# Two empty steps in the node stream of the last phase: one ahead of the second moments, one ahead of the shares

## The reference, cut to what matters

```python
out = agg.reshape(N, HEADS * HEAD_DIM) + xn @ W_res + bias
out = layer_norm(out, ln2_g, ln2_b)
ff = gelu_tanh(out @ ffn_w1 + ffn_b1) @ ffn_w2 + ffn_b2
x = x + out + ff                       # end of the attention layer
z = layernorm(x)
w = softmax(z @ Wr + br)               # shares of the 8 experts, per node
for e in experts:                      # h1, h2: relu(batchnorm(. @ W + b))
    y += w[:, e] * (h2(h1(z)) @ Wo[e] + bo[e])
x = x + y
```

## Time and profile before

| | |
|---|---|
| median of 3 runs | 3436.0 us (3429.38 to 3451.61) |
| the profiled execution | 3452.29 us, span 3450.7 us |
| mean granted TensorE clock | 0.898 of full speed |
| busy share of the span | PE 81%, DVE 64%, POOL 50%, ACT 44% |
| last phase | from about 1620 us to 3450.7 us |

### The profile page before, as it was taken

One profiled execution on the slowest core, in us unless ns is written; L12 is line 12 of the kernel. 1 busy time (PEld: TensorE's weight loads), 2 busy tenths in 40 slices (PEclk: granted clock), 3 DMA queues, 4 the chain that ended last, 5 costly groups with the idle time before them and its releaser, 6 DMA issues.

```text
span 3450.7 us, 51683 instructions
## 1 busy us (share of the span) xinstructions
PE 2781.1 (81%) x17241; PEld 2488.3 (72%) x17241; DVE 2193.0 (64%) x5199; ACT 1527.7 (44%) x2928; POOL 1731.8 (50%) x1691
## 2 busy tenths in 40 slices
PE   8468777677867777665468889999899999999998
PEld 7346666566756656565468888888788888898887
DVE  9424444444444444764567787887878878878754
ACT  5102222222222223333135656666566666566665
POOL 0466666656666654263555555555555445554200
PEclk9879988898889889687569899999999999999999
DMA  3645554545555544047657877777767768677544
GB/s 94 190 148 174 159 157 148 154 145 164 157 157 157 156 146 128 1 144 218 183 171 232 255 230 223 242 217 226 239 210 243 234 209 246 214 230 229 160 127 139
DMA packets 369271, 625.87 MB, mean 181 GB/s; under 512 B 86045, under 2 KB 237599, under 8 KB 368995
## 3 DMA queue, kind: packets, MB, share of 16 engines
q1 hardware_dynamic: 290659, 407.24, 37.2%
q0 software_dynamic: 75168, 211.78, 21.5%
q10 hardware_dynamic: 3168, 3.42, 0.3%
HBM read 508.86 MB, written 113.37 MB: 180 GB/s over the span
## 4 chain that ended last, share of the span: by engine, by line
PE 32%; DVE 12%; issue 6%; ACT 3%; DMA 1%; another core or an unknown queue 1%; SPq 0%; POOL 0%; DVEq 0%; ACTq 0%
PE PB L117 25%; DVE WGl L2443 2%; PE PB L2124 2%; PE PB L2126 2%; DVE G L2437 1%; PE PB L2139 1%; DVE XR L2616 1%; DVE H1l L2604 1%; ACT WGh L2290 1%; PE PB L2187 1%; DMA RI<-resd 1%; ACT TFm L2363 1%; DVE AR L2482 0%; DVE H2l L2604 0%
## 5 line engine op out<-in xcount | busy, mean ns | idle before, releaser
L2095 POOL DMA_INDIRECT G<-tab,SRCL x784 | 864.6, 1103 | 775.3 <-DVE WGl L2443 550.7
L900 POOL DMA_INDIRECT G<-tab,SRCL x782 | 768.4, 983 | 481.9 <-issue 224.5
L2363 ACT ACTIVATE TFm<-PB,BIA,SCL 128x512 f32<-128x512 f32 (+2 forms) x416 | 312.9, 752 | 241.6 <-PE PB L117 187.4
L932 PE MATMUL PB<-G,OR 128*128 128x257 f32 x782 | 272.8, 434 | 96.4 <-DMA G<-tab,SRCL 40.9
L2290 ACT CAST WGh<-G 128x1056 fp32r<-128x1056 f32 x196 | 210.4, 1073 | 290.8 <-DVE G L2437 144.4
L117 PE MATMUL PB<-H1h,MW 128*128 128x512 f32 (+2 forms) x832 | 297.8, 399 | 31.5 <-DVE H1l L2604 20.2
L117 PE MATMUL PB<-MW,H2h 128*128 128x256 f32 x1568 | 295.0, 286 | 16.6 <-DVE H2l L2604 14.0
L117 PE MATMUL PB<-YTMh,MW 128*128 128x512 f32 (+2 forms) x832 | 289.2, 397 | 1.3 <-ACT TF L2328 0.8
L2124 PE MATMUL PB<-WGh,OR 128*128 128x264 f32 x784 | 223.2, 310 | 59.2 <-DVE WGl L2443 32.5
L933 PE MATMUL PB<-G,OR 128*128 128x257 f32 x782 | 266.7, 426 | 0.0
L117 PEld LDWEIGHTS PB<-MW,H2h 128*128 128x128 f32 x1568 | 244.6, 191 | 23.5 <-DVE H2l L2604 14.8
(11 more groups left out here) (348 smaller groups left out, 7901.0 us busy)
## 6 DMA issues: line engine op xcount, KB each, us to landing
MW<-msplit SPq DMA_DIRECT2D x312, 512.0 KB
ord<-OR SPq DMA_DIRECT2D x392, 128.0 KB
OR<-ord SPq DMA_DIRECT2D x196, 256.0 KB
ROW<-relrow SPq DMA_DIRECT2D x196, 128.0 KB
G<-tab,SRCL POOLq DMA_INDIRECT x1566
msplit<-FWs SPq DMA_DIRECT2D x68, 256.0 KB
tab<-ACC SPq DMA_DIRECT2D x7, 896.0 KB, 7.4
resd<-RSG SPq DMA_DIRECT2D x49, 128.0 KB, 2.3
```

Of the source, the lines that this page charges most:

```text
L900: po.indirect_dma_start(b.G[:, u % RU, q, 0:256], None, c.tab0, bass.IndirectOffsetOnAxis(ap=c.SRCL[:, 2 * u + q:2 * u + q + 1].bitcast(U3 ...
L932: pe.matmul(PB[w % 2][:, 0:257], b.OR[:, u % RH, 0, :], b.G[:, u % RU, 0, :], start=first, stop=False)
L2095: po.indirect_dma_start(b.G[:, j % RP, u, :], None, c.tab1, bass.IndirectOffsetOnAxis(ap=c.SRCL[:, 4 * j + u:4 * j + u + 1].bitcast(U32), ...
L2363: a.activation(b.TM[:, m, 0:n], PB[of][:, 0:n], ACT.Relu, bias=b.BIA[:, l, q:q + 1], scale=b.SCL[:, l, q:q + 1]).then_inc(relu, 1)
```

## The change: two empty steps with a cost

`node_stream` gives two more steps called `rest`, one of cost 1.2 ahead of `mom2_a` and one of cost 1.0 ahead of the `pause` in front of `prepare` 4. No engine has an instruction for `rest`. The node stream's total cost for a group of four tiles rises by 2.2, so each of its other steps is a smaller share of it. `needed_by` does not know `rest`, so a follower is not put out ahead of it.

```diff
         if hh == 0 and nh == 2 and m == 5:
             yield ("turn_rows", h + 1), 0.5, (("rows_lo", h + 1),)
+    yield ("rest", g), 1.2, ()
     yield ("mom2_a", g), 0.8, ()
     yield ("mom2_b", g), 2.0, ()
     yield ("mom2_c", g), 0.5, ()
     ...
         if s == 4:
+            yield ("rest", g), 1.0, ()
             yield ("pause", g), 1.2, ()
```

## The result

The changed kernel takes 3419.7 us (median of 20 executions, 3407.0 to 3437.2), the kernel before 3436.4 (20 executions, 3424.7 to 3451.6) beside it: a ratio of 0.9944, 95% interval 0.9932 to 0.9957, or 17 us less (15 to 23 by the interval). The forecast was 42 less. The direction was right, but only two fifths of the gain came. The time lies in the stated range only because that range also takes in the rivals B and D; it lies above A's own range of 3376 to 3409.

A forecast was written before the change was run, and what follows sets the result against it. PE was taken to bound the last phase, but DVE the 60 us behind each `taken`; -45 + 4 + 3 - 4 = -42 us, from the median 3436.0 to 3394 us, range 3374 to 3428.

The forecast's parts named there:

- B: Rival: only the rest ahead of the second moments pays, ACT sets the wait at `share`; about -20 us, 3416; chance 0.21.
- D: Rival: E waits for gathers' data where `taken` waited, the 42 us come back but for some 10; 3426; chance 0.10.
- A: The forecast itself: the waits go, -42 us to 3394 us, own range 3376 to 3409; chance 0.62.
- What bounds the phase: Last phase: PE bounds the stretches between; DVE bounds the 60 us behind each `taken`, where PE stands still 81.4 us.
- The rest ahead of the second moments: Between the last HT9l and `taken`: DVE work put there takes 21 of `taken`'s 23.5 us wait for PE; bounds 0, 23.5.
- The second moments themselves: At RSTD: `mom2_b` ahead of a block's E and G in five groups takes 4 of 5.0 us wait; bounds 0, 5.
- The rest ahead of the shares: Between `logit` and `share`: DVE work put there takes 20 of the 28.3 us wait for the exponential; bounds 8, 28.
- The sum on DVE: 45 us less DVE idle time, each microsecond gained also PE's; 4 taken off for the first and last groups.
- What the earlier outputs cost: On PE, the last `output` now closer behind its `hidden`: 0.3 us in each of eleven groups, 3 us; bounds 0, 13.
- Clock: Behind PE's stops: fewer stops leave fewer microseconds at 1.2 GHz, giving 4 us, between 0 and 15.
- C: Rival: HT9l of a group's first and last pair comes too late for `output`, PE stops 63 us; 3457; chance 0.07.

The follow-up runs named there:

- the rest at the end: One rest of cost 2.2 as the node stream's last step, without the change's two rests, against the kernel before: ratios 0.9909, 0.9901, 0.9901, 0.9900.

## Why the prediction was wrong, step by step

- *What bounds the phase*: right in the place, too coarse in the cut. The 81.4 us of stops were one number for 60 us behind each `taken`; of PE's stops 41 us lie between `taken` and the biases' add and 41.5 in the head behind it, and only the former hang on the order round `taken` and `share`.
- *The rest ahead of the second moments*: the wait went as forecast, 23.0 us of 23.5. It bought nothing that can be told, and alone it costs 13 to 16 us. The charge had the wait in the wrong place: it ends where the 60 us begin (2419.82 us in the sixth group), so it is no part of DVE's 76.3 us of idle time there, and PE is busy 72.37 of the 72.40 us ahead of it.
- *The second moments themselves*: forecast 4 of 5.0 us gone. Counted with those that name the other root or nothing, the waits were 6.1 us and are 9.4 now (6.1, 2.0 and 1.3), in the first two groups and the last two above all.
- *The rest ahead of the shares*: 25.3 us of 28.3 went, more than the 20 charged. This rest carries the result: alone it gives 17 to 19 us. The table load's rows after read as the earlier trace rows: 1.28 us, with 0.02 us on either side. The rule that was weighed against them (the Trainium skill, ScalarE: Activation LUTs, What ACT_TABLE_LOAD costs) has 1.38 us of drain more, and by the prediction's estimate would have left 1.4 us at each share; the measured waits, 3.0 us at nine places, decide against it.

```profile
2428.07 1.07 ACT L2292 CAST WGh<-G 128x1056 fp32r<-128x1056 f32 x1
2429.16 1.28 ACT L2354 ACT_TABLE_LOAD   x1
2430.45 0.23 ACT L2354 ACTIVATE LG<-LG 128x32 f32<-128x32 f32 x1
```

- *The sum on DVE*: its idle time in the whole phase falls from 426 and 420 us to 383 and 389, 37 us, not far from the 45. **The step that failed is the next one**: "a microsecond that DVE gains is one that PE gains". PE's stops in the whole phase fall by 18 us for these 37, and in the regular stretch by 11 for some 30. By the time at which it lies, DVE's idle time falls by 17 us in the tail, and there PE's stops fall by 19. It falls by 31 in the middle, where PE had no stops to lose, and rises by 17 in the head, where PE's stops rise by 9. From the biases' add to the first `hidden` nothing is won: DVE is busy 289 of 302 us before, and 290 of 306 and 289 of 303 now. So a gain on DVE reached PE only up to DVE's next wait for the node chain, and only where PE was stopping for DVE.
- *The head's +9*: in the third and ninth group E waits 1.2 to 1.3 us for a releaser that the trace calls remote, and PE stops twice behind it; on a faster chip the ninth group has neither, and the head 45 us. In these two groups PE's stops are 4.7 and 6.5 us more than on the faster chip. So D, if remote stands for the gathers, has a small part, an estimated 5 to 7 us.

```profile
2865.87 0.22 DVE L2430 TENSOR_TENSOR E<-G,PB 128x64 f32<-128x64 f32 x1 [1.22 <-remote]
```

```profile
2868.46 0.47 PE L117 MATMUL PB<-YTMh,MW 128*128 128x512 f32 x1 [1.34 <-ACT TFm L2365]
2871.35 0.38 PE L117 MATMUL PB<-YT9h,GWh 128*128 128x256 f32 x1 [0.92 <-ACT TFm L2365]
```

- *What the earlier outputs cost*: charged 3 us; PE's waits for HT9l in the middle went from 2.2 to 6.6 us, while the others there, 5.4 us, went. The charge was right in size, but the middle as a whole does not stop PE more.
- *Clock*: forecast 4 us, too small. PE is busy 14 us less with the same matmuls (1344.9 and 1348.3 for 1361.9 and 1359.8). It was granted 1.2 GHz for 72 and 66 us of the regular stretch before and for 44 and 51 now; half of the difference, 10 us, is what the clock can have given back, 9 of it in the tail, where the stops fell. So the reason holds and the size was low: of the 25 us of the regular stretch 11 are stops and up to 10 the clock. Single traces scatter: half of the time at 1.2 GHz is 36 and 33 us before, 22 and 26 now, but 15 to 31 in the four traces with the rest at the end.
- *From the traces to the time*: the regular stretch gives 25 us, the first two `taken` lie 8 us closer (115 and 116 for 125 and 122), the last phase is 33 us shorter in all. But it began 9 us later in the mean (at 1622 and 1621 us after 1616 and 1608), and the medians differ by 17 (15 on the second chip). Part of that start is chance (below). The spans of the traced executions differ by 23, 7 more than the medians, because the first trace of before was an execution 16 us above its median.
- *The rivals*: B has it the wrong way round, the other rest pays, although its sign came (H1l and H2l wait 16 us longer for their casts). C did not come; D at most in two groups.

## What to carry to other kernels

Before you price a wait, ask which engine ends it next: idle time of the engine that waits is worth something only up to the next point where it waits for the bound engine anyway, so cut the profile at those points, not at round windows. Count PE's busy time along with its stops: with the same matmuls it moved by as much as they did. An empty step that puts work ahead of a wait takes that work from behind it; look first at what was covered there. And try the cheapest rearrangement, here a rest at the end, beside the aimed one.

## What the runs showed of the hardware

Ahead of the phase, in work that no order here touches, a row of small matmuls ran at 1.2 GHz in some executions and at 2.4 in others. Span, PE, PEld, DVE, ACT, POOL, clock; first before, then after:

```profile
1464.00:1474.00 10.00, 7.93 (x59) 7.10 (x58) 2.47 (x8) 4.37 (x14) 0.00 (x0) 0.98 0.00 0
```

```profile
1464.00:1478.00 14.00, 12.41 (x56) 11.81 (x56) 2.38 (x8) 4.00 (x12) 0.00 (x0) 0.50 0.00 0
```

In the 24 us ahead PE was busy 13.1 us at a granted clock of 0.64 in the former and 13.3 us at 0.59 in the latter. The same work took 10 us or 14, and the next matmul behind it starts 15.7 to 15.9 us after its first or 20.4 to 20.9. Of 19 traces 8 have the short time and 11 the long one, and the same kernel has both: the rest at the end 20.4, 20.5, 15.8 and 15.9 us; of before both traces are short, of both rests all three long. So 4.7 us of any pair of single traces of this kernel are a coin's throw.
